# Layer 1's attention scores as three F32R products of high and low halves, with a re-laid causal score stage and a merged end of layer 3, in a four-layer fp32 hybrid kernel

## The chip, the cores and the metric

The kernel runs on one core of one Trainium2 chip. The metric is the time on the device in microseconds, from one execution of the whole program. Three executions of the kernel before took 832.46, 831.14 and 831.80 us: the median is 831.8 us.

## What is computed

An input of 16 images of 96 channels and 256 pixels goes through four residual layers. In short form:

```python
x = x + L0(_gn(x))                       # super-token attention
x = x + L1(_gn(x))                       # attention with mixed heads
t = to_tokens(x)
t = t + causal_attn2(_ln_t(t)); t = t + quantised_ffn(_ln_t(t))
t = t + causal_attn3(_ln_t(t)); t = t + moe(_ln_t(t))
# L1, per image: 6 heads of 16 channels, 256 queries, 256 keys
scores = einsum('bhdq,bhdt->bhqt', q, k) * scale
mixed  = einsum('gh,bhqt->bgqt', head_w, scores)
attn   = softmax(mixed)
attn   = (attn - mean(attn)) * rsqrt(var(attn) + eps) * gamma + beta   # per image and head
out    = einsum('bhqt,bhdt->bhqd', attn, v)
# moe: gate = renormalised top 2 of softmax(x @ gate_w + gate_b), 4 experts
out = sum_e gate[e] * (gelu(x @ w1[e] + b1[e]) @ w2[e] + b2[e])
```

The two causal attentions have 6 heads of 16, with a mask above the diagonal, over the 256 tokens of each image.

## The kernel before, in words

Each engine has a program of its own, written out by hand: its order is the order of the code, and the engines meet through named semaphores (`wait_ge`, `then_inc`). Nothing is scheduled by a planner. B is 16 images, P is 128, TPI is 2 (token tiles to an image), NH is 6 heads. A **unit** is one pair of heads of one image: unit k = 3i + u, with i the image and u = 0, 1, 2.

**Layer 1** runs 48 units. For unit k TensorE issues the scores of unit k + 2 (`score_unit`, L961: four fp32 matmuls of 128x128 by 256 columns, each shown in the profile as two), then transposes the exponentials of unit k (L1201, eight of 128x128), then on even k weighs the values of four heads (`weigh_group`, L1048), on odd k transposes their outputs (`group_outputs`, L1056). In u = 0 it also projects queries and keys of image i + 2 (L992, L993); in u = 1 it waits in `parts_ready` until ScalarE has taken these out of PSUM bank 7, then adds up sums (L1081, L1082) and projects values of image i + 1 (L1006) into the same bank. VectorE takes the negated maxima of unit k + 2 (L1534, one reduce of 128x1024), then the statistics of the exponentials of unit k (L1702, four `bn_stats` of 256), then on odd k the division by the row sums (`normalise_group`, L1564 and L1566), and in u = 1 the variance and the values (L1610, L1611, L1557). ScalarE does the exponentials of unit k + 1 (L603), the copies of queries and keys (L613, L614) and the copies of the transposed exponentials (L590). GpSimd mixes the heads: it multiplies the queries by six columns of head weights (`mix`, L364, six of 96x256), and later sums squares (L400 to L406) and scales outputs (L414 to L419). The statistics of unit u = 0 wait for GpSimd's square sums.

The start of layer 1 is written out by hand as well: VectorE scales two weight matrices (L1651, L1652), takes group statistics in three portions (L1402) and two maxima; image 0 and 1 have three heads mixed by GpSimd and three by ScalarE (L619).

**Layers 2 and 3 (causal)** run the same units, two images written out and then a loop on the device over seven pairs of images. Queries and keys of image i + 2 are projected in u = 0 (L992, L993). ScalarE rounds them to a high half (L624), VectorE subtracts to get the low half (L1547), and SyncE stacks both halves with eight DMAs into the tile `qk` (L288). The scores are then F32R matmuls over 64 rows, one for each head of the pair and each of two query tiles (L968), of 128 and 256 columns, and two bf16 matmuls add the mask (L972). `weigh_values` (L1064) runs for three heads at the end of unit u = 2 and for the other three in the next unit u = 0, after the scores. In u = 0 VectorE copies the first half of the transposed exponentials (L1671), then makes the low halves, then copies the second half. The loops know no end: for the last images they still project, stack and score two images that don't exist (`LOOP_ADDS` counts them).

**The end of layer 3.** After the last image the outputs go back through transposes (L1015, L1022, L1029, L1036), layer norm of the last two images (VectorE, ScalarE L656, GpSimd L381 to L386) and a last transpose. Then, one after the other: 32 transposes of the residual (L1335) with ScalarE's copies (L812), 64 fp32 matmuls of 4 columns that give the gate's logits (L1340), the first three `hidden` steps of the experts (L1355), a wait for the gate (L1376), and the steady loop of 96 steps. A step is three F32R matmuls of 512 columns in (`hidden`, L1355), two Gelus on ScalarE (L829, L832), a subtraction on VectorE (L1882) and three F32R matmuls of 512 columns out (`expert_out`, L1366). The products of high and low halves are taken as high by high, high by low and low by high.

## Time and profile before

| What | Before |
|---|---|
| median of three executions | 831.8 us |
| the profiled execution's own time | 834.57 us |
| its span, first to last instruction | 832.4 us |
| TensorE matmul busy | 763.8 us, 92% |
| weight loads busy | 586.9 us, 71% |
| VectorE, ScalarE, GpSimd busy | 593.8, 576.5, 257.8 us |
| mean granted TensorE clock | 0.962 of full |

The profiled execution took 834.57 us, 2.2 us more than its span; it lies 2.8 us above the median. The granted clock is written as a share of full speed: 1.00 is 2.4 GHz and 0.50 is 1.2 GHz. In a timeline, a row gives start, length, engine, line, operation, what it writes and reads and how many instructions were merged; in square brackets stands how long the engine was idle before, and who ended that. Matmuls are pipelined, so a group's length includes the drain of its last one: the pace is read from the starts.

### The profile page before, as it was taken

What the parts mean: (1) busy time and instruction counts of PE and PEld (TensorE: products, weight loads), DVE (VectorE), ACT (ScalarE), POOL (GpSimd) and SP (SyncE); (2) the same over time, 40 slices, a digit from 0 to 9 for tenths busy, and PEclk for the clock granted to TensorE, in tenths of its full rate; (3) what the DMA queues carried; (4) which work ended last, traced back from release to release, by engine and by line L of the source; (5) the groups of instructions that cost most, each with busy time, mean ns of one, the idle gap of its engine ahead of it and who ended that gap; (6) DMA issues with size and microseconds to landing.
All of it is one profiled execution on the core that took longest, in us unless ns stands there. A gap on an engine that the chain in (4) does not pass through costs nothing.

```text
span 832.4 us, 17775 instructions
## 1 busy us (share of the span) xinstructions
PE 763.8 (92%) x5481; PEld 586.9 (71%) x5481; DVE 593.8 (71%) x1534; ACT 576.5 (69%) x1431; POOL 257.8 (31%) x505
## 2 busy tenths in 40 slices
PE   1997999999998989999998875999999978999997
PEld 1965877788786857777775674677777676777775
DVE  6146777777776667888875986678788716787775
ACT  2324878778777567878876754788888626877785
POOL 1802355656563441212111000222121201433334
PEclk9998999999999999999999985999999968999999
DMA  6000001011111223333321003223333203222320
GB/s 210 1 1 1 1 11 20 12 20 20 20 17 20 58 73 87 99 91 85 100 80 39 1 1 76 78 78 102 85 89 100 76 1 79 48 48 68 75 48 20
DMA packets 63271, 44.48 MB, mean 53 GB/s; under 512 B 34416, under 2 KB 55280, under 8 KB 63088
## 3 DMA queue, kind: packets, MB, share of 16 engines
q1 hardware_dynamic: 63216, 43.78, 21.1%
q8 instruction: 30, 0.49, 0.3%
q14 instruction: 25, 0.20, 0.1%
HBM read 12.24 MB, written 3.21 MB: 19 GB/s over the span
## 4 chain that ended last, share of the span: by engine, by line
PE 79%; DVE 12%; ACT 3%; issue 3%; POOL 1%; DMA 1%; POOLq 0%; SPq 0%; DVEq 0%
PE ps L1201 13%; PE ps L961 9%; PE ps L1366 8%; PE ps L1355 8%; PE ps L1064 6%; PE ps L968 5%; PE ps L972 4%; PE ps L992 3%; PE ps L1048 3%; PE ps L993 3%; PE ps L1006 3%; PE ps L1036 2%; PE ps L911 2%; PE ps L1015 1%; PE ps L1340 1%
## 5 line engine op out<-in xcount | busy, mean ns | idle before, releaser
L603 ACT ACTIVATE ee<-ps,nmax 128x128 f32<-128x128 f32 (+1 forms) x584 | 207.5, 444 | 8.5 <-DVE nmax L1534 5.1
L1201 PE MATMUL ps<-w,ee 128*128 128x128 f32 x960 | 140.6, 275 | 4.0 <-ACT big L590 1.5
L1201 PEld LDWEIGHTS ps<-w,ee 128*128 128x128 f32 x960 | 113.1, 143 | 21.0 <-ACT ee L603 7.2
L1537 DVE TENSOR_REDUCE nmax<-ps 128x2 f32<-128x256 f32 x200 | 101.8, 551 | 24.5 <-PE ps L972 23.6
L590 ACT ACTIVATE big<-ps 128x512 f32<-128x512 f32 (+1 forms) x192 | 97.6, 552 | 31.2 <-PE ps L1201 30.4
L1882 DVE TENSOR_TENSOR hhl<-ee,hhl 128x512 fp32r<-128x512 f32 x96 | 79.8, 837 | 31.2 <-ACT hhl L832 29.4
L961 PE MATMUL ps<-kh,big 128*128 128x256 f32 x384 | 94.7, 391 | 1.7 <-POOL big L364 1.2
L1534 DVE TENSOR_REDUCE nmax<-ps 128x4 f32<-128x1024 f32 x48 | 58.7, 1224 | 38.9 <-PE ps L961 38.4
L507 POOL TENSOR_TENSOR xc<-big,xc 96x512 f32<-96x512 f32 x32 | 53.0, 1657 | 107.5 <-DVE big L1876 107.3
L1355 PE MATMUL ps<-qk,w1hl 128*128 128x512 f32 x288 | 85.2, 407 | 0.4 <-DVE ee L1885 0.4
L1366 PE MATMUL ps<-hhl,w2hl 128*96 128x512 f32 x288 | 83.1, 399 | 0.3 <-DVE hhl L1882 0.3
L961 PEld LDWEIGHTS ps<-kh,big 128*128 128x128 f32 x384 | 70.3, 193 | 16.6 <-issue 3.7
L829 ACT ACTIVATE ee<-ps 128x512 f32<-128x512 f32 x96 | 57.5, 599 | 30.2 <-PE ps L1355 30.2
L364 POOL TENSOR_TENSOR big<-qs,w 96x256 f32<-96x256 f32 x90 | 52.0, 609 | 81.7 <-ACT qs L613 53.4
L1671 DVE COPY big<-ps 128x384 f32<-128x384 f32 x96 | 52.8, 550 | 31.0 <-PE ps L1201 31.0
L1702 DVE BATCH_NORM_STATS2 est<-ee 128x6 f32<-128x256 f32 x192 | 67.1, 412 | 5.0 <-POOL ssq L406 4.3
L381 POOL COPY onn<-tok 128x192 f32 (+1 forms) x31 | 10.7, 344 | 187.2 <-ACT lnr L658 187.2
L1355 PEld LDWEIGHTS ps<-qk,w1hl 128*128 128x128 f32 x288 | 55.9, 195 | 16.6 <-DVE ee L1885 0.6
L1366 PEld LDWEIGHTS ps<-hhl,w2hl 128*96 128x96 f32 x288 | 46.6, 162 | 19.1 <-issue 0.7
L832 ACT ACTIVATE hhl<-ps 128x512 fp32r<-128x512 f32 x96 | 57.1, 595 | 0.0
L1064 PE MATMUL ps<-big,vh 128*32 128x256 f32 (+1 forms) x792 | 56.1, 332 | 0.0
L968 PE MATMUL ps<-qk 64*128 64x128 f32 (+1 forms) x400 | 50.5, 331 | 1.5 <-ACT ee L603 1.5
(264 smaller groups left out, 1352.5 us busy)
## 6 DMA issues: line engine op xcount, KB each, us to landing
qk<-hl SPq DMA_DIRECT2D x288, 96.0 KB, 3.1
big<-moe_gate SPq DMA_DIRECT2D x8, 768.0 KB, 6.9
w<-w_in SPq DMA_DIRECT2D x1, 1735.0 KB, 13.3
xc<-x_in SPq DMA_DIRECT2D x4, 384.0 KB, 6.2
l_mix<-on SPq DMA_DIRECT2D x32, 48.0 KB, 2.1
tok<-l_mix SPq DMA_DIRECT2D x16, 96.0 KB, 2.0
out<-xc SPq DMA_DIRECT2D x8, 192.0 KB, 2.1
w<-w_in SPq DMA_DIRECT2D x1, 998.0 KB, 9.8
```

The lines of the kernel that those rows point to most:

```text
L590: nc.scalar.activation(et[:, h, 0:w], ps[:, 4 + hh, 0:w], ACT.Copy).then_inc(own(l, f"et{hh}"), 1)
L603: last = nc.scalar.activation(ee[:, ke, hh, qc, 0:w], src, ACT.Exp, bias=nmax[:, kp, hh, qc:qc + 1])
L961: last = mm(ps[:, 2 * kp + hh, qc * N:(qc + 1) * N], qh[:, par, 2 * u + hh, qc * P:(qc + 1) * P], kh[:, par, :], start=True, stop=True)
L968: mm(ps[:, 2 * kp + hh, qc * N:qc * N + w], qk[r0:r0 + 4 * HD, par, u, 0, qc * P:(qc + 1) * P], qk[r0:r0 + 4 * HD, par, u, 1, 0:w], start= ...
L1064: last = mm(ps[32 * r:32 * (r + 1), 6, g * N + q0:(g + 1) * N], vh[:, par, tc, 3 * g + r, :], et[:, 3 * g + r, tc * N:tc * N + N - q0], st ...
L1201: last = nc.tensor.transpose(ps[:, 4 + hh, b * P:(b + 1) * P], ee[:, u, hh, qc, tc * P:(tc + 1) * P], ident)
L1355: last = mm(ps[:, 4 + n % 4, :], w1hl[:, w, s * P:(s + 1) * P], xhl[:, t % 2, x, :], start=(k == 0), stop=(k == 2))
L1366: last = mm(ps[0:C, e, :], w2hl[:, w, s * C:(s + 1) * C], hhl[:, n % 4, h, :], start=(j == 0 and k == 0), stop=(j == NJ - 1 and k == 2))
L1534: last = V.tensor_reduce(out=nmax[:, kp, :, :].rearrange("p h q -> p (h q)"), in_=src, axis=AX.X, op=ALU.max, negate=True)
L1537: last = V.tensor_reduce(out=nmax[:, kp, :, qc], in_=ps[:, 2 * kp:2 * kp + 2, qc * N:qc * N + scores_cols(l, qc)], axis=AX.X, op=ALU.max, ...
L1702: last = V.bn_stats(est[:, par, q, 2 * u + hh, :], ee[:, u, hh, q, :])
L1882: V.tensor_tensor(hhl[:, n % 4, 1, :], hf[:, n % 4, :], hhl[:, n % 4, 0, :].bitcast(F32), ALU.subtract).then_inc(sg("moe_lo"), 1)
```

## The change

It does these things:

1. Layer 1's scores: GpSimd's mixed queries `qh` and ScalarE's keys `kh` are written as F32R (the high halves); VectorE makes the low halves (`keys_low`, one of 96x256 from PSUM for each image; `queries_low`, six of 96x256 for each image). The four fp32 matmuls of a unit become twelve F32R ones of 256 columns. `parts_ready` waits for the low keys as well, and ScalarE's queries wait for all low queries of the image before.
2. Layer 1's statistics: two `bn_stats` of 512 elements, which read two heads in turns, in place of four of 256; GpSimd's square sums lose one of seven operations. Some memsets of GpSimd in layer 0 go.
3. Causal scores: both heads of a pair share one stationary tile of 128 rows; the moving side holds the keys of one head over zeros and of the other under zeros, so that two F32R matmuls of 256 and 512 columns take the place of four of 64 rows. The two query tiles get a PSUM bank each.
4. Causal units: the work on images that don't exist goes; the first `weigh_values` moves from the end of u = 2 to the next u = 0, right before the second; VectorE's low halves come after both copies. The weights of queries and keys are laid out anew, and scaled in eight small pieces in place of two.
5. The end of layer 3: gate logits, residual transposes and the split of the first tokens are put between the last steps of the attention and the first steps of the experts; the Gelu table is loaded ahead; the gate's transpose comes at step 6, and the first gated sums come from step 14 on.

```diff
@@ score_unit
                 if l == 1:
+                    pe.wait_ge(sg("l1_qlo"), NH * (k // 3) + 2 * u + 2)
                     for hh in range(2):
                         for qc in range(TPI):
-                            last = mm(ps[:, 2 * kp + hh, qc * N:(qc + 1) * N], qh[:, par, 2 * u + hh, qc * P:(qc + 1) * P],
-                                      kh[:, par, :], start=True, stop=True)
+                            q, out = (slice(qc * P, (qc + 1) * P), ps[:, 2 * kp + hh, qc * N:(qc + 1) * N])
+                            mm(out, qh[:, par, 2 * u + hh, q], kh[:, par, :], start=True, stop=False)
+                            mm(out, qh[:, par, 2 * u + hh, q], kl[:, par, :], start=False, stop=False)
+                            last = mm(out, ql[:, par, 2 * u + hh, q], kh[:, par, :], start=False, stop=True)
                 else:
+                    for qc in reversed(range(TPI)):
+                        w = scores_cols(l, qc)
+                        mm(both(kp, qc, w), qk[:, par, 3 + u, qc * P:(qc + 1) * P], qk[:, par, u::6, 0:w], start=True, stop=False)
                     for qc in range(TPI):
                         w = scores_cols(l, qc)
-                        for hh in range(2):
-                            r0 = hh * 4 * HD
-                            mm(ps[:, 2 * kp + hh, qc * N:qc * N + w], qk[r0:r0 + 4 * HD, par, u, 0, qc * P:(qc + 1) * P],
-                               qk[r0:r0 + 4 * HD, par, u, 1, 0:w], start=(qc == 0), stop=False)
-                    for hh in range(2):
-                        diag = ps[:, 2 * kp + hh, :].rearrange("p (b t) -> p b t", t=P)[:, 0::3, :]
-                        last = mm(diag, identb[:, :], mid_dim(maskb[:, :], 1, TPI), start=False, stop=True)
+                        last = mm(both(kp, qc, w)[:, :, w - P:w], identb[:, :], mid_dim(maskb[:, :], 1, 2), start=False, stop=True)
@@ parts_ready
-                for what in ("q_sb", "k_sb") if l == 1 else ("hi", "lo"):
+                for what in ("q_sb", "k_sb", "klo") if l == 1 else ("hi", "lo"):
@@ vector engine
+            def keys_low(n, par):
+                dve.wait_ge(sg("l1_k_sb"), n + 1)
+                V.tensor_tensor(kl[:, par, :], ps[0:C, 7, N:2 * N], kh[:, par, :].bitcast(F32), ALU.subtract).then_inc(sg("l1_klo"), 1)
+            def queries_low(n, par, heads):
+                if n >= 2:
+                    dve.wait_ge(sg("l1_s_ps"), 3 * n - 3)
+                for g in heads:
...
+                    V.scalar_tensor_tensor(out=ql[:, par, g, :], in0=qs[:, :], scalar=wa("l1_hw", C)[:, g:g + 1], in1=qh[:, par, g, :].bitcast(F32),
+                                           op0=ALU.mult, op1=ALU.subtract).then_inc(sg("l1_qlo"), 1)
...
                     group_stats(range(4, 8))
+                    keys_low(0, 0)
                     values(l, 0, 0)
+                    queries_low(0, 0, range(NH))
...
                     group_shift("gn1b")
+                    keys_low(1, 1)
+                    queries_low(1, 1, range(NH))
...
-                        for hh in range(2):
-                            for q in range(TPI):
-                                last = V.bn_stats(est[:, par, q, 2 * u + hh, :], ee[:, u, hh, q, :])
+                        for q in range(TPI):
+                            last = V.bn_stats(est[:, par, q, u, :], ee[:, u, :, q, :].rearrange("p h t -> p t h"))
                         last.then_inc(sg("l1_est"), 1)
+                    if l == 1 and u == 1 and i + 2 < B:
+                        keys_low(i + 2, par)
+                    if l == 1 and u == 2 and i + 2 < B:
+                        queries_low(i + 2, par, range(0, NH // 2))
+                    if l == 1 and u == 0 and 1 <= i < B - 1:
+                        queries_low(i + 1, npar, range(NH // 2, NH))
@@ scalar engine, queries
                     if not isinstance(n, int) or n > 0:
-                        act.wait_ge(sg("l1_qmix"), n)
+                        act.wait_ge(sg("l1_qmix"), all_mixed(n - 1))
+                        act.wait_ge(sg("l1_qlo"), NH * n)
@@ causal units: vector engine, u == 0
                         copy_probs(0)
-                        keys(l, i + 2, par, i // 2 + 1 if isinstance(i, int) else it + 1)
                         copy_probs(1)
+                        if before(i + 2, B):
+                            keys(l, i + 2, par, i // 2 + 1 if isinstance(i, int) else it + 1)
@@ causal units: tensor engine, u == 0
                         for hh in range(2):
                             pe.wait_ge(*upto(l, f"et{hh}", START + k))
+                        if l == 3 or not isinstance(i, int) or i > 0:
+                            pe.wait_ge(*upto(l, "oc", i))
+                            pe.wait_ge(*upto(l, "v_sb", i))
+                        weigh_values(l, npar, 0)
                         weigh_values(l, npar, 1).then_inc(own(l, "av"), 1)
@@ end of layer 3, tensor engine
+                    if l == 3:
+                        pe.wait_ge(*upto(l, "max", 3 * B))
+                        pe.wait_ge(*upto(l, "exp", 6 * B))
+                        gate_logits(0)
                     outputs(l, B - 1)
...
+                    gate_logits(1)
...
+                    residual_rows(0)
...
+                    for g in range(2, 6):
+                        gate_logits(g)
+                    residual_rows(7)
                     image_back(l, B - 1, 1)
+                    gate_logits(6)
+                    gate_logits(7)
...
             for n in range(LAG):
                 hidden(n)
-            pe.wait_ge(sg("f3_gate"), 1)
-            nc.tensor.transpose(ps[:, 0, P:2 * P], gate[:, 0, :, :].rearrange("p t e -> p (t e)"), ident).then_inc(sg("moe_gate_ps"), 1)
-            pe.wait_ge(sg("moe_gate_t"), 1)
+                residual_rows(n + 1)
             for n in range(LAG, NS * NB):
                 hidden(n)
                 expert_out(n - LAG)
+                if n < 6:
+                    residual_rows(n + 1)
+                if n == 6:
+                    pe.wait_ge(sg("f3_gate"), 1)
...
@@ end of layer 3, scalar engine
+                    residual_channels(0)
+                if l > 1:
                     outputs_by_channel(l, B - 1)
                 if l == 3:
...
+                    split_high(0)
+                    split_high(1)
                     deviation(l, B - 1, 1)
+                    residual_channels(7)
...
+            nc.scalar.preload_act_table_set("gelu_and_others")
+            residual_channels(1)
```

`residual_rows(g)` is the four transposes (before L1335) and `residual_channels(g)` ScalarE's copy (before L812). In the new gate code VectorE's first two subtractions of the experts stand between the steps of the gate.

## Rows read from the trace of the kernel before

**Rows 1.** The profile's page, part 1: busy time, share of the span, instructions.
```profile
PE 763.8 (92%) x5481; PEld 586.9 (71%) x5481; DVE 593.8 (71%) x1534; ACT 576.5 (69%) x1431; POOL 257.8 (31%) x505
```
**Rows 2.** Stages: length, busy PE, PEld, DVE, ACT, POOL (instructions), clock, DMA, GB/s.
```profile
160.00:200.00 40.00, 40.00 (x297) 32.43 (x297) 30.16 (x74) 30.82 (x87) 25.25 (x67) 1.00 0.11 17
...
740.00:780.00 40.00, 40.00 (x173) 29.88 (x172) 31.66 (x41) 32.15 (x61) 16.25 (x10) 1.00 0.24 52
```
**Rows 3.** Timeline of layer 1, starts of the scores in unit u = 1.
```profile
168.32 1.89 PE L961 MATMUL ps<-kh,big 128*128 128x256 f32 x8
...
172.02 0.46 PE L1081 MATMUL ps<-w,big 96*128 96x96 f32 x2
...
191.91 0.38 PE L961 MATMUL ps<-kh,big 128*128 128x256 f32 x1
```
**Rows 4.** Timeline of layer 1, the next unit u = 1 and what follows.
```profile
180.17 1.41 DVE L1702 BATCH_NORM_STATS2 est<-ee 128x6 f32<-128x256 f32 x4 [0.96 <-POOL ssq L406]
...
180.61 1.99 PE L961 MATMUL ps<-kh,big 128*128 128x256 f32 x8
...
182.44 1.04 PE L1201 MATMUL ps<-w,ee 128*128 128x128 f32 x8
182.65 1.23 DVE L1534 TENSOR_REDUCE nmax<-ps 128x4 f32<-128x1024 f32 x1 [1.07 <-PE ps L961]
...
183.54 0.36 PE L1081 MATMUL ps<-w,big 96*128 96x96 f32 x2
...
183.79 1.40 DVE L1702 BATCH_NORM_STATS2 est<-ee 128x6 f32<-128x256 f32 x4
...
184.40 1.92 PE L961 MATMUL ps<-kh,big 128*128 128x256 f32 x8
...
187.13 1.07 PE L1048 MATMUL ps<-big,vh 128*32 128x256 f32 x16
```
**Rows 5.** One line's instructions (ns min/median/max); then groups of lines by shape.
```profile
L1882 DVE TENSOR_TENSOR hhl<-ee,hhl x96: 671/692/1777, 692.1 to 825.6; 128x512 fp32r<-128x512 f32 x96
```
```profile
L1702 DVE BATCH_NORM_STATS2 est<-ee 128x6 f32<-128x256 f32 x192 | 67.1, 412 | 5.0 <-POOL ssq L406 4.3 <-ACT ee L603 0.7
```
**Rows 6.** Timeline of the start of layer 1.
```profile
66.05 0.69 PE L1006 MATMUL ps<-w,xn 128*128 128x96 f32 x4
...
67.00 3.54 DVE L1652 TENSOR_SCALAR w<-w 128x96 f32<-128x96 f32 x1
...
72.32 1.23 DVE L1534 TENSOR_REDUCE nmax<-ps 128x4 f32<-128x1024 f32 x1
```
**Rows 7.** Timeline of layer 3, one image in the loop; then the stacking DMAs.
```profile
602.12 0.67 PE L992 MATMUL ps<-xb,w 128*96 128x256 f32 x2
...
604.14 0.49 PE L968 MATMUL ps<-qk 64*128 64x128 f32 x4
...
604.57 0.39 PE L972 MATMUL ps<-maskb,identb 128*128 128x256 bf16 x2
...
605.32 0.31 PEld L1201 LDWEIGHTS ps<-w,ee 128*128 128x128 f32 x3 [0.27 <-issue]
```
```profile
DMA to landing us min/median/max: 3.0/3.1/3.2
```
**Rows 8.** Timeline of the end of layer 3 and the first steps of the experts.
```profile
660.68 1.59 PE L1064 MATMUL ps<-big,vh 128*32 128x256 f32 x24
...
669.63 0.63 PE L1029 MATMUL ps<-w,onn 128*96 128x128 f32 x2 [3.75 <-POOL onn L386]
...
676.42 9.93 PE L1340 MATMUL ps<-w,xn 128*128 128x4 f32 x64 [0.83 <-ACT xc L812]
...
687.37 1.28 ACT L829 ACT_TABLE_LOAD   x1
...
698.90 0.86 PE L1355 MATMUL ps<-qk,w1hl 128*128 128x512 f32 x3
```
**Rows 9.** A stage of the gate logits, columns as in rows 2.
```profile
682.00:684.00 2.00, 2.00 (x11) 2.00 (x10) 0.00 (x0) 0.00 (x0) 0.00 (x0) 0.50 0.00 0
```

272 lines of the change are left out of this document (162 added, 110 removed).

## The prediction

> **What bounds the kernel now.** I began with the page's busy line [rows 1]: TensorE's matmuls are busy 763.8 of 832.4 us and no other engine passes 71%, so TensorE bounds the whole. Busy hides pace and waits, though, so I read the stages [rows 2]. In layer 1 TensorE is busy 40.0 of 40 us at full clock, VectorE 30.2 of 40. The start of the unit u = 1 scores gives the length of one image there: 168.32, 180.61, 191.91 [rows 3, 4], thus 12.29 and 11.30 us by parity, mean 11.8. VectorE has 40 - 30.2 = 9.8 us in 40 to spare, 2.9 an image. That is what layer 1 can pay with, and the change asks more of it.
>
> **Layer 1, TensorE.** A score unit runs from 180.61 to the next group's start at 182.44: 1.83 us for eight profile entries [rows 4]. No F32R product of 256 columns stands in layer 1. The experts give the pace of one of 512: 173 matmuls in a busy 40 us, 0.231 each [rows 2]. Taking off 256 columns at 2.4 GHz (0.107) leaves 0.125; the lower bound is 0.107, the upper half the slow case, 0.216 (half-unit entries of today, 1.73/8). I take 0.127, near the F32R row: twelve cost 1.52 against 1.73 to 1.83. Saved: 0.2 to 0.3 a unit; with 0.21, 48 units give -10 us if nothing else waits.
>
> **Layer 1, the low keys.** TensorE's sums (L1081) use the bank in which the keys lie, and must now wait for `keys_low`. On VectorE that comes behind the maxima of the scores just made and the statistics. Today the scores end at 182.60 (180.61 + 1.99), the maxima start at 182.65 and the statistics at 183.79, while TensorE reaches the sums at 183.54 [rows 4]. Today's four statistics run 1.40 together, 412 ns each if alone [rows 4, 5]; two over the same 1024 elements save two starts. The maxima pass 1024 elements in 1.14 (183.79 - 182.65) [rows 4]. I take 1.19 (the lower bound 1.14, the upper 2.8 if the strided read runs at half pace). `keys_low`, 256 columns from PSUM, I put at 0.40: between half of the 512-column subtraction (0.692/2 = 0.346 [rows 5]) and the statistics' 0.412. So the low keys are ready 1.14 + 1.19 + 0.40 = 2.7 us, with handovers 2.8, after the scores end: 185.4 against 183.54, 2.0 us of waiting (with shorter scores a little less). In the other parity TensorE weighs values first: scores end about 170.2, sums start 172.02 [rows 3], so 1.0 us. Mean 1.5 us an image.
>
> **Layer 1, the low queries.** Six an image at about 0.34 (half of 0.692 [rows 5]; the lower bound a quarter of the maxima's 1.14, 0.28; the upper half of 1.777, 0.89). That makes 2.0 us, and with the keys 2.4, less 0.2 from the statistics: 2.2 of the 2.9 us spare. On the busy account it fits; in the order of the queue it does not quite. Laid out by hand from one `keys_low` to the next (all of it VectorE and TensorE in turn): sums and values 0.86 (184.40 - 183.54), scores 1.62, transposes 0.87, weighing 1.0, scores to their end 1.8, handover 0.1, maxima 1.14, statistics 1.19, three low queries 1.02, maxima 1.14, statistics 1.19, low keys 0.40: 12.3 us, and 11.5 in the parity without weighing at that place. The wait for GpSimd's square sums, 0.96 an image [rows 4], stays in the middle of it, and the division by the row sums in one parity. GpSimd's squares lose one operation of seven, which would take some tenths off it; I count nothing, since the mixing ahead of them on GpSimd now starts later. That makes about 13.1 against 11.8: +1.3 an image, over 14 images +18 us, which already contains the scores' gain. The lower bound is the wait alone: 1.5 x 14 - 10 = +11; and if half of it is hidden, 0.
>
> **Layer 1, ScalarE's queries.** The copy of queries now waits until all six low queries of the image before are made. The last three stand in VectorE's queue of unit u = 0 behind the statistics, which end at 181.58 (180.17 + 1.41) [rows 4], so until 182.6. Behind this copy wait the keys' copy, the copies of transposed exponentials and the next exponentials on ScalarE, and on GpSimd the mixing of that image. TensorE's sums want the keys' copy at 183.54 and the low keys want it at 185.0: it costs nothing as long as VectorE is less than about 1 us late; beyond that every microsecond goes on to the sums. The mixing has a whole image until its scores.
>
> **Layer 1, its start.** Values of image 0 (L1006) start at 66.05, and now wait for the low keys, in a bank that VectorE can't touch before its scaling of weights is over: 67.00 + 3.54 = 70.54 [rows 6]. Then six low queries (2.0 us) stand ahead of the maxima (72.32), and again for image 1. Some hides behind the group statistics: +5 us (3 to 7). Layer 1 in sum: +23.
>
> **Causal layers.** A unit's four score matmuls run from 604.14 to 604.57, 0.43 us [rows 7]; two of 512 and 256 columns should take 0.231 + 0.127 = 0.36: -0.07, three times an image -0.2. Weighing all heads in u = 0, with the second half of the transposed exponentials copied ahead of the low halves, lets go the 0.27 us idle before the transposes' loads [rows 7]. That is -0.45 an image, over 26 images in mid-loop -12. The low halves now come later, and behind them SyncE's eight transfers, whose landing alone takes 3.1 us [rows 7]: I keep -10. For images that don't exist, projections (0.67 each [rows 7]) and two score units a layer go, about 2.9 us, half of it hidden: -1.5 a layer. Sum: -13 (bounds -4, if the transfers come late every image, and -16). The eight small weight scalings stand in place of two, in one layer's gaps; with 0.28 to 0.41 for a short operation they cost VectorE at most six more, 2 us, once. I count nothing: a single delay inside layer 1 is within its bounds.
>
> **The end of layer 3.** Weighing ends at 662.27 (660.68 + 1.59); step 6 of the experts, the first after the gate, starts at 698.90: 36.6 us [rows 8]. Between lie 3.75 us of idling on GpSimd, 0.83 on a copy, 9.93 us of logits at half clock (0.50 [rows 9]), a table load of 1.28, the gate. After it, idle stretches are filled with logits and transposes; the table load and most of the gate leave the path. Worked out, step 6 comes some 20 us after the weighing: 9.9 (logits, half as long at full clock, 5 us, and in gaps) + 3.75 + 1.28 + 0.83 = 15.8 even before the gate's own wait. I take -16 (bounds -8 and -20). Here stands my main doubt: in these rows the engine runs at half clock when it idles between small matmuls, and no row shows that many small ones in the gaps keep it up.
>
> **Sum.** +23 - 13 - 16 = -6. The profiled execution of 834.6 goes to 828.6; the median lies 2.8 below that execution, so 831.8 - 6 = 826.
>
> **The rivals.**
> 1. *Slower: the low queries are slow, and the queue turns.* Each reads two operands from SBUF while GpSimd mixes heads. The subtraction of the same kind takes 0.692 in the median but up to 1.777 [rows 5], and a 96-column scaling took 3.54 us with GpSimd at work [rows 6]. With 0.6 in place of 0.34, six cost 1.6 us more an image, of which about 1.1 is on the path: 14 x 1.1 = +16, thus 842. It decides from about 0.44 a piece on: six times 0.1, two thirds of it on the path, are +0.4 an image and eat the 6 us. Against it: in layer 1 GpSimd is busy 25.3 of 40 us [rows 2], and the maxima read PSUM. The Trainium skill ("SBUF — State Buffer", section "SBUF: two separate sides") says that VectorE's operations with two SBUF inputs and GpSimd's that read SBUF take a shared port pair as an exclusive lock for a whole instruction. By that rule alone each low query may wait out a mix, so it speaks for this rival; the spread 692 to 1777 agrees, no row shows how often it happens.
> 2. *Faster: layer 1 stays at TensorE's pace.* If the low keys come early enough and only the 10 us count, with +5 at the start: -5 - 13 - 16 = -34, thus 798; with 7 us of waits left, 805. For it: 2.9 us of spare VectorE an image. Against: the maxima stand directly ahead in VectorE's queue.
> 3. *No change: the entry stays at half clock.* With 10 in place of 16, and one microsecond less in the causal layers: 832.
> 4. *The cheap product isn't cheap.* If an F32R product of 256 columns costs 0.216 as an fp32 entry does, a unit takes 12 x 0.216 = 2.59 and the change doesn't do what it is made for. The chain above holds two score units, each 1.0 longer: 15.1 against 11.8, thus 14 x 3.3 = +46, +5 at the start, -29 from the other parts: +22, about 854. Against: the 0.231 for 512 columns [rows 2].
>    A strided statistics read at half pace (2 x 1.6 more an image on VectorE) would end in the same place.
>
> **How the numbers follow.** Forecast 0.45, slow low queries 0.22, TensorE's pace 0.10, no change 0.14, dear products or statistics 0.09. The forecast's own range is 815 to 832 and lets 0.07 fall within 0.2% (1.7 us, about what a measurement of this kernel tells from none: 830.1 to 833.5) and 0.02 beyond it; the third rival is spread too, 0.07 within it, 0.04 above, 0.03 below. Faster: 0.36 + 0.10 + 0.03, about 0.50; same 0.14; slower: 0.22 + 0.09 + 0.04 + 0.02, about 0.36. The range leaves out the dear case and rival 2, 0.19 in all: 808 to 850.
>
> **What would show it.** In layer 1 the starts of u = 1 scores should lie 13.0 apart in the mean, with TensorE idle 1 to 2 us before the sums, the end put down to VectorE's low keys; a score unit 1.5 us; low queries 0.34 at the median; two statistics 1.2 together. In a causal loop an image should be shorter by 0.4. From the last weighing to step 6 some 20 us. I am wrong if the idle before the sums is absent (then the time falls toward 800), if low queries stand at 0.5 or more, or if the clock stays at 0.50 through the first steps of the experts.

## The result: 862.1 us, slower by 3.6%

The kernel after took 862.08 us (median of 4 executions, 861.62 to 863.95), the kernel before on the same chip 832.13 us (831.14 to 833.95). The ratio is 1.036, with a 95% interval from 1.034 to 1.0379. The forecast was 826, from 808 to 850: wrong in direction, and outside its range by 12 us. The profiled execution has a span of 860.5 us against 832.4.

The profile's page of the kernel after, busy times (part 1) and the line of the granted clock in 40 slices (part 2):

```profile
PE 765.1 (89%) x5457; PEld 614.2 (71%) x5457; DVE 620.2 (72%) x1542; ACT 574.3 (67%) x1419; POOL 250.5 (29%) x483
...
PEclk9997878888888799999999999589999988999999
```

Beside [rows 1] TensorE is busy for nearly the same time (765 us), now of a longer span, VectorE for 26 us more, and the clock line shows a stretch of eights where layer 1 is. The stages tell it plainly. First the kernel after, one row for the steady part of layer 1; then the 14 us of one image (columns as in [rows 2]: length, busy PE, PEld, DVE, ACT, POOL, clock):

```profile
100.00:310.00 210.00, 182.33 (x1383) 160.39 (x1382) 156.92 (x316) 132.39 (x343) 89.50 (x239) 0.84 0.08 13
```
```profile
180.00:184.00 4.00, 1.18 (x11) 0.94 (x9) 4.00 (x9) 1.78 (x5) 2.06 (x4) 0.91 0.00 0
184.00:186.00 2.00, 1.87 (x9) 1.90 (x10) 0.33 (x2) 0.00 (x0) 1.41 (x3) 0.50 0.00 0
186.00:188.00 2.00, 2.00 (x11) 2.00 (x11) 0.59 (x3) 1.44 (x6) 0.70 (x4) 0.50 0.00 0
188.00:190.00 2.00, 2.00 (x11) 2.00 (x11) 1.23 (x2) 0.80 (x3) 1.76 (x5) 0.50 0.00 0
190.00:192.00 2.00, 2.00 (x25) 1.19 (x24) 2.00 (x5) 1.85 (x6) 0.84 (x4) 0.97 0.46 49
...
194.00:196.00 2.00, 2.00 (x17) 1.82 (x16) 2.00 (x5) 1.98 (x6) 0.00 (x0) 1.00 0.00 0
```

In [rows 2] the clock of layer 1 is 1.00 (the kernel before had 1.00 from 100 to 262 us too). Now TensorE does almost nothing for 3 us, and then works without a pause, but at 0.50, the lower of its two levels (1.2 GHz), for over 6 us; only then is it at 2.4 GHz again. The timeline of the same stretch (start, length, engine, line, operation):

```profile
179.92 1.04 PE L1268 MATMUL ps<-w,ee 128*128 128x128 f32 x8
...
180.80 0.38 PE L1099 MATMUL ps<-w,ots 128*128 128x128 f32 x2
181.17 1.21 DVE L1607 TENSOR_REDUCE nmax<-ps 128x4 f32<-128x1024 f32 x1
...
182.31 1.29 DVE L1810 BATCH_NORM_STATS2 est<-ee 128x6 f32<-128x512 f32 x2
183.52 0.40 DVE L1617 TENSOR_TENSOR hl<-ps,hl 96x256 fp32r<-96x256 f32 x1
...
184.13 0.71 PE L1125 MATMUL ps<-w,big 96*128 96x96 f32 x2 [2.96 <-issue]
...
185.83 0.56 PE L1005 MATMUL ps<-hl,qhr 96*128 96x256 f32 x1
186.19 0.41 PE L1006 MATMUL ps<-hl,qhr 96*128 96x256 f32 x1
186.40 0.41 PE L1007 MATMUL ps<-hl,w1hl 96*128 96x256 f32 x1
...
188.54 1.80 PE L1268 MATMUL ps<-w,ee 128*128 128x128 f32 x8
...
191.27 0.39 PE L1005 MATMUL ps<-hl,qhr 96*128 96x256 f32 x1
...
192.68 0.28 PE L1007 MATMUL ps<-hl,w1hl 96*128 96x256 f32 x1
...
192.79 1.04 PE L1268 MATMUL ps<-w,ee 128*128 128x128 f32 x8
```

The sums (L1125, before L1081) wait until VectorE has made maxima, statistics and low keys (L1617), as foreseen. The view labels that idling "issue", so the releaser is read from the order of events: L1617 ends at 183.92 and the sums start at 184.13, and in each of the twelve images with such a wait they start 0.21 us after the low keys. The score unit after it takes 188.54 - 185.83 = 2.71 us, the next one 192.79 - 191.27 = 1.52 us. One line's waits, for the whole of layer 1:

```profile
L1125 PE MATMUL ps<-w,big x32: 244/275/498, 123.6 to 328.4; 96*128 96x96 f32 x32
its engine sat idle before it (us, times) until:
  issue: 51.4, 24
```

Matmuls and weight loads are counted apart here, 12 times each, so an image idles about 2 us (TensorE's matmuls by themselves: 1.54 us in every other image, 1.91 to 2.96 in those between); in the kernel before the same line had 2.5 us in 6 times, all of them before weight loads.

Where the 28.1 us of the span are, by starts of the same work in both traces: the first sums 110.9 before, 123.6 now (+12.7); eleven images later 242.8 and 291.9 (15.30 an image in place of 11.99: +36.4); the first scores of layer 2 298.9 and 347.6 (+48.7 in all); layer 2 up to the first matmul of its feed-forward 144.7 and 139.0 (-5.7); that feed-forward 76.6 and 75.2 (-1.4); layer 3 to its last weighing 141.8 and 135.2 (-6.6); from there to the last `hidden` 162.0 and 155.0 (-7.0). Of these last two stretches the eight traces of this document with the changed kernel's end of layer 3 untouched (its own and seven variants of layer 1) give 133.4 to 135.2 and 153.4 to 155.0 us: differences of 1 to 2 us there mean nothing.

### The profile page after: what moved, and what is told of

Its sections match the earlier page's. It is cut to its first block, busy times and chain, and to the rows that moved or that the text cites. A ratio compares the mean times of both kernels' runs of the same rounds, so it can differ in the third digit from the quotient of the medians.

```text
span 860.5 us, 17551 instructions
## 1 busy us (share of the span) xinstructions
PE 765.1 (89%) x5457; PEld 614.2 (71%) x5457; DVE 620.2 (72%) x1542; ACT 574.3 (67%) x1419; POOL 250.5 (29%) x483
## 4 chain that ended last, share of the span: by engine, by line
PE 63%; DVE 12%; issue 7%; ACT 3%; POOL 1%; POOLq 0%; DVEq 0%; ACTq 0%
PE ps L1268 9%; PE ps L1418 8%; PE ps L1433 8%; PE ps L1107 6%; PE ps L1011 4%; PE ps L1049 3%; PE ps L1005 2%; PE ps L1035 2%; PE ps L1014 2%; PE ps L1007 2%; PE ps L1006 2%; PE ps L1036 2%; PE ps L1091 2%; ACT ee L632 2%; DVE est L1810 2%
## 5 line engine op out<-in xcount | busy, mean ns | idle before, releaser
L632 ACT ACTIVATE ee<-ps,nmax 128x128 f32<-128x128 f32 (+1 forms) x576 | 204.7, 440 | 20.4 <-DVE nmax L1607 13.4
L1268 PE MATMUL ps<-w,ee 128*128 128x128 f32 x960 | 145.5, 289 | 2.0 <-ACT big L619 1.9
L1268 PEld LDWEIGHTS ps<-w,ee 128*128 128x128 f32 x960 | 120.6, 151 | 8.9 <-ACT ee L632 2.8
L1610 DVE TENSOR_REDUCE nmax<-ps 128x2 f32<-128x256 f32 x192 | 97.4, 549 | 12.9 <-PE ps L1014 8.3
L392 POOL TENSOR_TENSOR qhr<-qs,w 96x256 fp32r<-96x256 f32 x90 | 52.1, 612 | 117.3 <-ACT qs L643 88.6
L1778 DVE COPY big<-ps 128x384 f32<-128x384 f32 x96 | 50.2, 551 | 36.1 <-PE ps L1268 36.1
L1005 PE MATMUL ps<-hl,qhr 96*128 96x256 f32 x192 | 67.2, 350 | 0.6 <-ACT ee L632 0.3
L1810 DVE BATCH_NORM_STATS2 est<-ee 128x6 f32<-128x512 f32 x96 | 62.6, 693 | 3.9 <-POOL ssq L433 3.2
L409 POOL COPY onn<-tok 128x192 f32 (+1 forms) x31 | 11.1, 360 | 184.6 <-ACT lnr L688 184.6
L1011 PE MATMUL ps<-qk 128*128 128x512 f32 x192 | 59.9, 394 | 3.1 <-ACT ee L632 1.7
L1006 PE MATMUL ps<-hl,qhr 96*128 96x256 f32 x192 | 61.9, 322 | 0.0
L1007 PE MATMUL ps<-hl,w1hl 96*128 96x256 f32 x192 | 61.8, 322 | 0.0
```

The lines of the kernel that those rows point to most:

```text
L632: last = nc.scalar.activation(ee[:, ke, hh, qc, 0:w], src, ACT.Exp, bias=nmax[:, kp, hh, qc:qc + 1])
L1005: mm(out, qh[:, par, 2 * u + hh, q], kh[:, par, :], start=True, stop=False)
L1006: mm(out, qh[:, par, 2 * u + hh, q], kl[:, par, :], start=False, stop=False)
L1007: last = mm(out, ql[:, par, 2 * u + hh, q], kh[:, par, :], start=False, stop=True)
L1011: mm(both(kp, qc, w), qk[:, par, 3 + u, qc * P:(qc + 1) * P], qk[:, par, u::6, 0:w], start=True, stop=False)
L1268: last = nc.tensor.transpose(ps[:, 4 + hh, b * P:(b + 1) * P], ee[:, u, hh, qc, tc * P:(tc + 1) * P], ident)
```

## The experiments

Two theories stood against each other. **Clock**: TensorE's waiting, new in layer 1, sends its clock to half, and that doubles what the wait itself costs. **Queue**: VectorE's in-order chain, longer by the low halves, sets the pace; the clock only goes down because TensorE has nothing to hurry for.

### The low keys ahead of the maxima

```diff
@@ VectorE, unit
+                    if l == 1 and u == 1 and i + 2 < B:
+                        keys_low(i + 2, par)
                     if before(k + 2, 3 * B):
                         maxima(l, k + 2, j % 2)
...
-                    if l == 1 and u == 1 and i + 2 < B:
-                        keys_low(i + 2, par)
```

> One move against the changed kernel: VectorE makes the low keys ahead of the maxima of unit u = 1, not behind the statistics. Nothing else differs, no work is taken away. Clock theory (TensorE idles 1.5 to 3 us before the sums, its clock then falls to half and the next two units run at 1.2 GHz): the idle before the sums goes, the granted clock in layer 1 is 1.00, VectorE's own busy time (about 11.6 us an image) sets the pace, the sums come 12.2 us apart in place of 15.3, 14 images give -43: about 819. Queue theory (VectorE's in-order chain of maxima, statistics and low queries sets the pace, the clock only follows): 13.1 us an image, about 831. If neither the wait nor the clock matters: 862.

Measured: 824.26 us (ratio to before 0.9893, 0.9867 to 0.9919). One line moved takes 38 us off: the kernel is no longer 3.6% slower than the one before but 1.1% under it. The stage of layer 1 in this kernel:

```profile
100.00:270.00 170.00, 153.44 (x1344) 130.32 (x1342) 152.76 (x308) 125.39 (x335) 89.79 (x234) 0.97 0.10 15
```

The sums are 12.50 us apart in the mean (12.2 from the fourth image on), VectorE is busy 153 of 170 us, 90%, and TensorE as much. The first images still see half clock; 12.50 and not 12.2 over eleven images is 3 of the 5 us by which the expected 819 was missed. This settles that the place of the low keys matters, but it took the wait and the low clock away together; the next run separates them.

### Needless matmuls while it waits

```diff
@@ TensorE, u == 1
+                        if l == 1 and i + 2 < B:
+                            pe.wait_ge(*upto(l, "exp", 2 * k + 4))
+                            for _f in range(20 if i % 2 == 0 else 10):
+                                mm(ps[:, 2 * ((j + 1) % 2), 0:N], kh[:, npar, 0:P], kh[:, npar, :], start=True, stop=True)
                         if before(i + 2, B):
                             parts_ready(l, i + 2)
```

> The changed kernel, and in place of idling before the low keys TensorE does 20 (even images) or 10 (odd) needless F32R products of 256 columns into a score bank that is overwritten afterwards. The wait for the low keys stays; only TensorE's idleness goes. Clock theory: granted clock 1.00 in layer 1, the two units after the sums lose their 3 us of half pace, 12.5 to 13.0 us an image, total 825 to 832, although work was added. Queue theory: the chain through VectorE is as long as before, so 862 or, with the added work, a few us more.

Measured: 836.89 us (1.0046, 1.0027 to 1.0065), 25 us less than the changed kernel, with more work in it. Its stage, and the fill in its timeline:

```profile
100.00:286.00 186.00, 175.08 (x1560) 152.60 (x1559) 154.56 (x312) 128.51 (x342) 92.48 (x240) 1.00 0.09 14
```
```profile
186.17 1.46 PE L1287 MATMUL ps<-hl 96*128 96x256 f32 x10
187.81 0.43 PE L1125 MATMUL ps<-w,big 96*128 96x96 f32 x2 [0.18 <-issue]
...
188.69 0.37 PE L1005 MATMUL ps<-hl,qhr 96*128 96x256 f32 x1
188.89 0.28 PE L1006 MATMUL ps<-hl,qhr 96*128 96x256 f32 x1
...
190.19 1.04 PE L1268 MATMUL ps<-w,ee 128*128 128x128 f32 x8
```

From TensorE's last needful matmul to the sums it is 1.57 us in one parity and 2.25 to 3.04 in the other, no less than without the fill, and the sums still start 0.2 to 0.4 us after the low keys. The scores (190.19 - 188.69 = 1.50 us) run at 2.4 GHz, and the sums come 13.51 us apart. So the 3.32 us an image that layer 1 lost are 1.53 us of waiting and queue (13.51 - 11.99) and 1.79 us of half clock (15.30 - 13.51). The queue theory alone, which asked for 862, is out; the clock theory's 825 to 832 was 5 us too low, since the images take 13.1 to 14.2 us and not 12.5 to 13.0.

### The scores taken back

```diff
@@ score_unit
-                            mm(out, qh[:, par, 2 * u + hh, q], kh[:, par, :], start=True, stop=False)
-                            mm(out, qh[:, par, 2 * u + hh, q], kl[:, par, :], start=False, stop=False)
-                            last = mm(out, ql[:, par, 2 * u + hh, q], kh[:, par, :], start=False, stop=True)
+                            last = mm(out, qh[:, par, 2 * u + hh, q].bitcast(F32), kh[:, par, :].bitcast(F32), start=True, stop=True)
...
-                        keys_low(i + 2, par)
...
-                        queries_low(i + 2, par, range(0, NH // 2))
...
-                        queries_low(i + 1, npar, range(NH // 2, NH))
```

> The changed kernel with layer 1's scores taken back: four fp32 matmuls a unit, no low keys or queries, no waits for them; the two-in-turns statistics, the causal layers and the end of layer 3 stay as changed. Both theories: layer 1 lasts as before (the first scores of layer 2 at about 299 us in place of 347.6), so 862 - 48.7 = 813, two us less if the shorter statistics count. It says what the rest of the change is worth: some -19 against the kernel before. If the statistics or the causal layers also cost time, it is above 820.

Measured: 810.01 us (0.9722, 0.9696 to 0.9748), 24 us below the 833.6 of the kernel before that ran beside it; no later kernel is faster beyond noise. The sums are 11.97 us apart, as before the change (11.99), although VectorE's two strided statistics replaced four: they were neither dear (1.29 us the pair) nor of use, because TensorE is at 161 of 162 us there:

```profile
100.00:262.00 162.00, 160.78 (x1198) 129.89 (x1200) 118.13 (x217) 124.81 (x336) 85.98 (x235) 1.00 0.11 17
```

### fp32 products with all the waits kept

```diff
@@ score_unit
-                            mm(out, qh[:, par, 2 * u + hh, q], kh[:, par, :], start=True, stop=False)
-                            mm(out, qh[:, par, 2 * u + hh, q], kl[:, par, :], start=False, stop=False)
-                            last = mm(out, ql[:, par, 2 * u + hh, q], kh[:, par, :], start=False, stop=True)
+                            last = mm(out, qh[:, par, 2 * u + hh, q].bitcast(F32), kh[:, par, :].bitcast(F32), start=True, stop=True)
```

> The changed kernel with only the twelve F32R products of a unit replaced by four fp32 matmuls of the high halves; the low halves are still made and waited for, but left out of the scores. If the F32R products themselves are what is dear: much faster than 862, 830 or less. Clock theory: the waits are the same, the clock falls as before, and fp32 matmuls (1.73 us a unit at full clock, 3.5 at half) run longer than the twelve (1.4 and 2.55), so slower still, 870 to 885. Queue theory: about 0.3 us a unit more, 870.

Measured: 850.71 us, one execution, so without an interval; it lies 11 us below the four of the changed kernel (861.62 to 863.95), and no theory foresaw it. Stage and waits of this kernel:

```profile
100.00:300.00 200.00, 173.43 (x1224) 138.75 (x1222) 157.19 (x314) 131.90 (x347) 91.42 (x240) 0.97 0.09 13
```
```profile
  issue: 48.0, 24
```

TensorE idles before the sums nearly as long as in the changed kernel (48.0 us in 24 against 51.4 in 24), yet the clock stays at 0.97. The sums are 14.46 us apart; most images take 13.6 to 14.5, and the three in which the clock fell take 15.3, 15.8 and 16.9. The waits ahead of those three were 2.25, 1.55 and 2.24 us, and others of 2.25 and of 2.54 us passed without a fall. So my clock theory was too simple: idling of this length doesn't send the clock down by itself. What differs from the changed kernel is that the work between two waits is longer by 0.2 to 0.3 us a unit. The last run takes this up.

### Half of the low queries

```diff
@@ score_unit
-                            last = mm(out, ql[:, par, 2 * u + hh, q], kh[:, par, :], start=False, stop=True)
+                            last = mm(out, (ql if 2 * u + hh < 3 else qh)[:, par, 2 * u + hh, q], kh[:, par, :], start=False, stop=True)
@@ VectorE, unit
-                        queries_low(i + 1, npar, range(NH // 2, NH))
```

> The kernel with the low keys made first (the run before, 824), and of the low queries only heads 0 to 2 are made; the third product of heads 3 to 5 takes the high half instead, so these low halves are left out of the result, with as many matmuls. VectorE loses 3 x 0.41 = 1.2 us an image. If VectorE's load sets layer 1's pace once the clock is up (36 of 40 us busy), the sums come 11.0 to 11.3 us apart in place of 12.2: 14 images and the start give -14, about 810. If TensorE or GpSimd sets it: 822 or more.

Measured: 810.68 us (0.9723, 0.9699 to 0.9747), 13.6 below the run at 824. Not all of that is pace: the start, too, makes three low queries an image in place of six, and the first sums come 5.4 us earlier (112.0 against 117.4). The rest is: the sums are 11.70 apart in the mean in place of 12.50, 11.1 to 11.7 in the later images, with as many matmuls, so TensorE was not the limit at 12.2. (Part of the mean is clock again: the fall in the first images is gone.) It also bounds what F32R brings in this order of work: even with three of six low queries gone, the whole only draws level with four fp32 matmuls (810.01).

### The start of layer 1

```diff
@@ VectorE, start of layer 1
-                    for name in ("l2", "l3"):
...
-                            V.tensor_scalar(v, v, QS, None, ALU.mult).then_inc(sg(f"{name}_wq"), 1)
-                    group_stats(range(4, 8))
                     keys_low(0, 0)
+                    group_stats(range(4, 8))
```

> The kernel with the low keys made first, and at the start of layer 1 the low keys of image 0 come ahead of VectorE's statistics, and the sixteen small weight scalings wait until images 3 and 5. TensorE's 6.4 us of idling before the values of image 0 should go, nearly. Expected -4 to -6 against 824: 819. If the first maxima and low queries only wait for something else (ScalarE, the later statistics): within 1 us of 824.

Measured: 819.08 us (0.982, 0.9795 to 0.9845), 5 us below the run without it. There are eight of the small scalings, four for each causal layer (the sixteen above is a slip). In the changed kernel the start reads as follows: the eight before the low keys, and TensorE waiting for these keys.

```profile
64.86 3.79 DVE L1755 TENSOR_SCALAR w<-w 128x16 f32<-128x16 f32 x8
...
70.46 1.14 PE L1049 MATMUL ps<-w,xn 128*128 128x96 f32 x4 [6.36 <-DVE hl L1617]
```

In the mended kernel the same wait is 1.32 us. The first sums come at 112.3 in place of 117.4; the fp32 kernel has them at 109.2.

### The logits at the end of layer 3, with larger matmuls between

```diff
@@ gate_logits
                     last = mm(ps[:, 0, t * NE:(t + 1) * NE], xn[:, t * P:(t + 1) * P], wa("f3_gate"), start=True, stop=True)
+                    if g in (2, 3, 4, 5, 6, 7):
+                        mm(ps[:, 4, 0:N].rearrange("p (b t) -> p b t", t=P), identb[:, :], mid_dim(maskb[:, :], 1, TPI), start=True, stop=True)
```

> The changed kernel with one needless bf16 product of 256 columns put behind each of 48 logit matmuls of 4 columns in the end of layer 3. Clock theory: the half clock in the stretch from the logits to the third step of the experts (13 us at 0.50) comes from TensorE doing only matmuls of 4 columns; with the larger ones between, the clock stays up, the stretch gets 5 to 6 us shorter less 4 to 5 us of added work: 862 - 1, and a granted clock above 0.9 there. If the clock falls because of the idling ahead of the logits: 0.50 as before, and 48 x 0.2 = 10 us more, 872.

Measured: 859.73 us, from 852.74 to 865.17: too wide to show a gain. (The edit puts in 24 matmuls: each of the 24 logit products is two of the 48 profile entries.) The profiled execution was the one of 852.74. There, 8 us around the logits; under it the same stretch of the changed kernel:

```profile
698.00:702.00 4.00, 3.89 (x45) 3.89 (x46) 2.53 (x8) 1.59 (x5) 1.04 (x2) 1.00 0.00 0
702.00:706.00 4.00, 4.00 (x44) 3.80 (x43) 0.96 (x3) 0.59 (x1) 0.72 (x2) 1.00 0.02 4
```
```profile
700.00:704.00 4.00, 3.26 (x22) 3.01 (x20) 1.89 (x8) 2.37 (x6) 0.00 (x0) 0.76 0.00 0
704.00:708.00 4.00, 4.00 (x20) 4.00 (x20) 0.64 (x2) 0.03 (x1) 1.77 (x3) 0.50 0.00 0
...
712.00:716.00 4.00, 4.00 (x15) 3.41 (x16) 2.33 (x11) 2.17 (x4) 0.00 (x0) 0.53 0.00 0
```

At full clock the same engine gets twice as many matmuls through (44 against 20 in 4 us), and from the last weighing to the last `hidden` it took 148.5 us against 155.0. In the other executions the whole run's granted clock was lower, 0.924 to 0.934 against 0.939 in this one; layer 1's share in that can't be told from a run without a trace. That matmuls of 4 columns suffice for the fall, without idling among them, the kernel before shows: its logits start at 676.42, and 4 us into them, with TensorE busy throughout, the clock falls.

```profile
678.00:680.00 2.00, 2.00 (x20) 2.00 (x20) 0.31 (x1) 0.00 (x0) 0.00 (x0) 1.00 0.00 0
680.00:682.00 2.00, 2.00 (x15) 2.00 (x14) 0.00 (x0) 0.00 (x0) 0.00 (x0) 0.68 0.00 0
```

### The gate earlier, alone and with its sums

```diff
@@ TensorE, steps of the experts
-                if n == 6:
+                if n == 4:
                     pe.wait_ge(sg("f3_gate"), 1)
@@ VectorE
-                if n == 4:
+                if n == 2:
                     dve.wait_ge(sg("moe_gate_ps"), 1)
```

> The changed kernel with the gate's transpose after step 4 of the experts and not after step 6, VectorE's copy of it after its second low half. The gates come to the sums 3 to 3.6 us earlier, and TensorE's stall of 1.93 us before the first sum that needs them, with the half clock behind it (0.62 over the next 4 us), goes: 862 - 3.7 = 858.4. If the stall has another cause, 862.

Measured: 859.75 us (857.23 to 866.18), and in its trace the stall is still there, 1.92 us. In the changed kernel it looked like this, with a half clock behind it:

```profile
738.70 0.90 PE L1433 MATMUL ps<-hhl,w2hl 128*96 128x512 f32 x3 [1.93 <-DVE big L1987]
739.44 1.30 PE L1418 MATMUL ps<-qk,w1hl 128*128 128x512 f32 x3
```
```profile
736.00:740.00 4.00, 2.07 (x9) 1.38 (x8) 3.21 (x5) 1.58 (x4) 1.19 (x1) 0.96 0.00 0
740.00:744.00 4.00, 4.00 (x12) 2.83 (x12) 1.35 (x2) 1.80 (x4) 2.18 (x3) 0.62 0.00 0
```

The releaser was named rightly, the first gated sum (L1987); but what that sum waited for was not the gates' arrival. The second run also moves the first sum (L1987) forward in VectorE's queue:

```diff
@@ gate_step
-            return max(NJ * k + 6, 14 + k)
+            return max(NJ * k + 6, 12 + k)
```

> The changed kernel with the gate's transpose after step 4 and, new, the gated sums from step 12 on in place of 14 (so in front of two low halves and a split that stand ahead of the first sum in VectorE's queue). If the stall of 1.9 us before the fourth group of output matmuls comes from that place in VectorE's queue and not from the gate's arrival, it goes now: last weighing to last hidden step 151 to 152 us in place of 154.9. If it comes from the gate's transfer: it stays at 1.9 us or grows.

Measured: 861.02 us (1.0341, 1.0323 to 1.0359). The stall is gone, so with the gate early its sum's place in VectorE's queue was the cause. From step 6 to the last `hidden` the trace takes 125.8 us against 128.9. The whole gains 1.1 us against the changed kernel, which can't be told from nothing: from the last weighing to the last `hidden` it is 153.5 us, 1.5 less, not the 3 expected, because in this execution the half clock of the logits lasted longer, from 702 to 719 us in place of 702 to 716.

### The best of both ways

```diff
@@ the run "scores taken back", gate_logits
+                    if g in (2, 3, 4, 5, 6, 7):
+                        mm(ps[:, 4, 0:N].rearrange("p (b t) -> p b t", t=P), identb[:, :], mid_dim(maskb[:, :], 1, TPI), start=True, stop=True)
@@ gate_step
-            return max(NJ * k + 6, 14 + k)
+            return max(NJ * k + 6, 12 + k)
...
-                if n == 6:
+                if n == 4:
                     pe.wait_ge(sg("f3_gate"), 1)
```

> Layer 1's scores taken back to four fp32 matmuls (the run at 810), with the needless matmuls between the logits and the earlier gate and sums. Layer 1 ends as in that run; last weighing to last hidden step 145 to 147 us in place of 153.5: 801 to 804.

Measured: 809.53 us (0.9729, 0.9703 to 0.9754), from 804.99 to 812.50. Its five executions fall in two groups: 804.99 and 806.64 at a mean granted clock of 0.977 and 0.974, and 809.53, 810.48 and 812.50 at 0.965 or 0.966. The profiled execution is the 804.99: there the clock stays at 1.00 through the logits, and from the last weighing to the last `hidden` it is 147.0 us, as expected. That it falls in the second group is likely but was not traced. As a median it is no faster than the fp32 kernel without them (810.01).

```diff
@@ the run "start of layer 1", with the same edits
...
-            return max(NJ * k + 6, 14 + k)
+            return max(NJ * k + 6, 12 + k)
```

> The F32R scores with the low keys first and the mended start of layer 1 (the run at 819), with the same end of layer 3 as the kernel beside it: 810 to 813. If it comes out below the fp32 one, the F32R products pay in layer 1 after all; I expect it 8 to 10 us above, since VectorE is busy 36 of 40 us there.

Measured: 817.58 us (0.9805, 0.9779 to 0.9832). The F32R way, with everything mended that I found, stays 8 us above the fp32 way. In the two traces 6.4 us of it are there by the first scores of layer 2 (302.7 against 296.4), although this trace idles before the sums hardly more than 0.8 us and keeps its clock in layer 1 after the first images. This trace also shows the larger matmuls failing to hold the clock between the logits, with the same code as in the 804.99:

```profile
660.00:664.00 4.00, 4.00 (x28) 4.00 (x29) 1.10 (x2) 0.46 (x2) 1.76 (x3) 0.50 0.00 0
```

### More work, the wait untouched

```diff
@@ score_unit, layer 1
                     pe.wait_ge(sg("l1_qlo"), NH * (k // 3) + 2 * u + 2)
+                    for _f in range(4):
+                        mm(ps[:, 2 * kp, 0:N], kh[:, par, 0:P], kh[:, par, :], start=True, stop=True)
```

> The changed kernel, waits and order untouched, with four needless F32R products ahead of the scores of every unit of layer 1: more work for TensorE, 1.4 us an image at full clock, and the idling before the sums stays (it isn't filled). If the length of that idling alone sends the clock down: granted clock 0.80 to 0.86 as before and 2 us more an image, 880 to 890. If the clock goes by how busy TensorE is over a longer stretch: it stays near 1.00 and the sums come about 14 us apart in place of 15.3, so faster than 862, 845 to 850, although nothing but work was added.

Measured: 855.92 us (1.0291, 1.0273 to 1.0308), 6 us faster than the changed kernel by nothing but 192 needless matmuls. Stage and waits:

```profile
100.00:300.00 200.00, 176.45 (x1548) 154.52 (x1548) 157.12 (x316) 130.81 (x343) 90.07 (x240) 0.97 0.08 13
```
```profile
  issue: 44.0, 24
```

TensorE still idles 44.0 us in 24 times, 1.8 us each (2.1 in the changed kernel), and the clock is 0.97, not 0.84. The sums are 14.55 us apart: 15.5 in the three images in which the clock fell, 14.0 to 14.7 in the rest, where the changed kernel has a fall in every image. Of the two outcomes written down it is nearer to the second, but 6 us short of its 845 to 850. Together with the fp32 run it says that not the wait alone but also how much TensorE does around it decides whether the clock falls: faster products leave less work between the same waits. That is my reading of two runs, one of them a single execution and the other with waits a little shorter; why the clock falls in one image and not in the next, neither shows. The Trainium skill ("TensorE: Matmul & The Clock Gate", section "Part 1: The HAM clock gate (the "warmup" mystery)") says the same of the mechanism, that the level is set by how busy the engine has been recently; these runs agree, 0.84 against 0.97 with nearly equal waits.

## Why the prediction was wrong, point by point

**Layer 1's bound: right.** TensorE did set the pace before (161 of 162 us), and VectorE's spare time is what the change spent: with the clock up (the run at 824) VectorE is busy 90%.

**The F32R product: right at 2.4 GHz.** 12 x 0.127 = 1.52 us was forecast for a unit and 1.52 measured (191.27 to 192.79). At 1.2 GHz the same unit took 2.71, longer than the fp32 unit's 1.83 [rows 4].

**The wait for the low keys: right.** 2.0 and 1.0 us by parity were forecast; 1.91 to 2.96 and 1.54 came in the trace, and no less with the clock held up by needless work (2.25 to 3.04 and 1.57), so each is about half a microsecond longer than forecast. 13.1 us an image was the forecast of the queue, and with the clock held up it measures 13.51: +1.5 in place of +1.3.

**The step that failed** is the sum of the chain itself: "laid out by hand from one `keys_low` to the next". Every TensorE term in it (0.86, 1.62, 0.87, 1.0, 1.8) was taken at full clock from rows in which TensorE never waited, while the same text put a wait of 1 to 2 us into each image in front of them. So half clock in layer 1 was a term put at nothing, without a reason. It adds 1.79 us an image: the forecast was +1.3, the chip gave +3.32, thus +36.4 us over the eleven images between the first sums and the twelfth, where the forecast asks for 14. I had named the half clock as a doubt for the end of layer 3 [rows 9], though misread (TensorE is busy 2.00 of 2 us in that row, it doesn't idle between the small matmuls), and didn't ask whether the new wait would bring it into layer 1.

**The start of layer 1: the term was mis-sized.** +5 was forecast, +12.7 at the first sums measured. The first wait came as it was priced: the values of image 0 start at 70.46, and 70.54 was forecast. (The trace had been 2.0 us ahead of the one before until then, the first projections of layer 1 at 61.19 against 63.21, so the wait is 6.36 us.) The weight scalings that stand in VectorE's queue ahead of the low keys took 3.79 us, hardly more than the 3.66 of the two of before (66.88 to 70.54). Apart from the first two of the eight they are long, and all of that beside GpSimd's multiplications and memset; in the run that moved them to where GpSimd is idle, none took over 0.2 us:

```profile
L1755 DVE TENSOR_SCALAR w<-w x8: 177/2447/3527, 64.9 to 66.7; 128x16 f32<-128x16 f32 x4, 128x32 f32<-128x32 f32 x4
```
```profile
L1813 DVE TENSOR_SCALAR w<-w x8: 149/166/182, 123.4 to 148.9; 128x16 f32<-128x16 f32 x4, 128x32 f32<-128x32 f32 x4
```

That run, with the low keys ahead of the statistics as well, gave 5 us back. What the term left out is the way from the values of image 0 to the first sums, 53.1 us in place of 44.9: in it lie waits for the low keys of the next images (1.85, 1.34 and 1.91 us) and half clock again (0.75 over 66 to 100 us, 0.90 before). The low keys ahead of the maxima brought the first sums from 123.6 to 117.4.

**The causal layers: nearly right.** -13 forecast, -5.7 and -6.6 measured. An image of the loop now reads:

```profile
599.86 0.67 PE L1035 MATMUL ps<-xb,w 128*96 128x256 f32 x2
...
601.74 0.60 PE L1011 MATMUL ps<-qk 128*128 128x512 f32 x2
602.17 0.39 PE L1014 MATMUL ps<-maskb,identb 128*128 128x256 bf16 x2
...
608.22 0.67 PE L1035 MATMUL ps<-xb,w 128*96 128x256 f32 x2
```

8.36 us long, 8.38 in the mean of both parities, where the loop of before has 8.70: 0.32 less, and 0.45 was forecast. Its scores take 0.43 here, where 0.36 was forecast, as long as the four of before [rows 7]. So the saved score time never came; the 0.27 us idle before the transposes' loads did go. How much the images that don't exist gave, no run shows.

**The end of layer 3: mis-sized.** -16 forecast. Weighing ends at 697.35 (695.85 + 1.50) and step 6 starts at 723.12: 25.8 us against 36.6, so -10.8 at that point. My bounds named the reason, the clock stayed at half from 702 to 716 us, through the logits and the first two steps of the experts. Another 3.9 us were lost behind step 6 (128.9 us to the last `hidden`, 125.1 before): there lie a stall of 1.93 us that I hadn't seen (the first gated sum stands behind a low half and a split in VectorE's queue) and the half clock that followed, and without both, in the run with the earlier sum, it is 125.8. That makes -7 in the end.

**The rivals.** "The low queries are slow" was given 0.22, with 842. It had the right sign and the wrong mechanism. They took 0.41 apiece and not 0.34, which costs 0.4 us an image, but were never slow:

```profile
L1628 DVE SCALAR_TENSOR_TENSOR w1hl<-qs,w,qhr x96: 458/474/484, 71.9 to 303.8; 96x256 fp32r<-96x256 f32 x96
```

458 to 484 ns over 96 of them: what the shared port pair of the Trainium skill ("SBUF — State Buffer", section "SBUF: two separate sides") would have added doesn't show in this kernel. But it is hardly put to the test: an instruction of GpSimd runs beside only 8 of the 96. With the low keys first it is 23, of which five took 689 to 703 ns while the median stayed at 474, so such a delay is rare here, not absent; and the weight scalings above, up to 3527 ns beside GpSimd's work, show how large it can be. "The cheap product isn't cheap" (0.09 with the strided statistics) came true for a part of the time, as the unit of 2.71 us at half clock, for a reason that it didn't name; and its price, some 854 us, was nearest to the result.

## What to carry to other kernels

When a change gives the bounding engine a wait that it didn't have, price the wait and the matmuls behind it at both levels of the clock; here the second term (1.79 us an image) was larger than the first (1.53). Cheaper matmuls can make that worse, since less work stands between the same waits (one execution with fp32 products and all the waits was 11 us faster), so the operand that unlocks TensorE belongs first in VectorE's queue: one moved line was worth 38 us. And where needless matmuls in a wait make a kernel faster (862 to 837 us here), it is paying for the clock: a cheap test.

## What was unexpected on the chip

Nearly equal idling gave different clocks: 51.4 us in 24 waits with a clock of 0.84, but 48.0 and 44.0 us in 24 waits with 0.97, when TensorE's work between was longer. The opposite came too: TensorE was busy for 4.00 of 4 us at 0.50, with nothing but matmuls of 4 columns, from 704 to 708 us, and 24 larger ones in between kept it at 1.00 in two traced executions and not in a third, a difference of some 6.5 us in that stretch (147.0 and 148.5 us against 153.9). That is most of the spread of the kernel that took 804.99 to 812.50 us, if its slower executions, which weren't traced, differ in this. What exactly tips it stays open; no run here measures it.
